# Last attention's scores in three fp32r passes instead of one fp32 product, with query and key split

## The reference, cut to what matters

```python
Q = query @ Wq + bq
K = key @ Wk + bk
V = value @ Wv + bv
Q = Q.reshape(B, S, NUM_KV, GROUPS, HEAD_DIM).transpose(0, 2, 3, 1, 4)
...
scale = 1.0 / jnp.sqrt(jnp.asarray(HEAD_DIM, query.dtype))
scores = jnp.einsum('bhgqd,bhkd->bhgqk', Q, K) * scale
w = jax.nn.softmax(scores, axis=-1)
y = jnp.einsum('bhgqk,bhkd->bhgqd', w, V)
...
return y @ Wo + bo
```

## Time and profile before

| what | us |
|---|---|
| median of 3 runs | 1620.5 (1618.6 to 1621.03) |
| the profiled execution, its own time | 1619.05 |
| span of the profiled execution | 1617.3 |
| the last attention, from its first key product to the last product with the values | about 1398 to 1567 |

### The profile page before, as it was taken

One profiled execution on the slowest core, in us unless ns is written; L12 is line 12 of the kernel. 1 busy time (PEld: TensorE's weight loads), 2 busy tenths in 40 slices (PEclk: granted clock), 3 DMA queues, 4 the chain that ended last, 5 costly groups with the idle time before them and its releaser, 6 DMA issues.

```text
span 1617.3 us, 25912 instructions
## 1 busy us (share of the span) xinstructions
PE 1572.8 (97%) x8958; PEld 1264.1 (78%) x8958; DVE 981.2 (61%) x2633; ACT 742.1 (46%) x2151; POOL 399.3 (25%) x278
## 2 busy tenths in 40 slices
PE   8999999999999999999989999999999999899997
PEld 7888888888888888888875877868696788666556
DVE  6762663626636356363676774848576767756677
ACT  5442443424434244343433462735355332288873
POOL 3131320313203132032204300000001343376651
PEclk9999999999999999999999999999999999999999
DMA  5111111101111011110224000000001613000001
GB/s 179 54 43 34 59 45 41 42 29 55 42 52 42 29 55 42 52 43 30 79 79 195 14 1 14 0 13 0 0 1 41 223 52 107 14 14 14 1 1 53
DMA packets 34436, 76.22 MB, mean 47 GB/s; under 512 B 5569, under 2 KB 18497, under 8 KB 32193
## 3 DMA queue, kind: packets, MB, share of 16 engines
q1 hardware_dynamic: 34368, 75.36, 14.1%
HBM read 73.25 MB, written 2.10 MB: 47 GB/s over the span
## 4 chain that ended last, share of the span: by engine, by line
PE 78%; DVE 10%; ACT 5%; issue 3%; DVEq 2%; POOL 1%; DMA 1%; POOLq 0%; SPq 0%; ACTq 0%
PE banks L1183 11%; PE banks L1128 10%; PE banks L1101 9%; PE banks L1109 9%; PE banks L1333 9%; PE banks L1437 5%; PE banks L1239 4%; PE banks L1222 3%; PE banks L1409 3%; ACT p L978 2%; PE banks L1229 2%; PE banks L1540 2%; PE banks L1563 1%; PE banks L1357 1%; PE banks L1547 1%
## 5 line engine op out<-in xcount | busy, mean ns | idle before, releaser
L1183 PE MATMUL banks<-w_o,atT 128*128 128x512 f32 x720 | 180.2, 396 | 0.0
L527 POOL TENSOR_TENSOR w_q<-w_raw_q,w_q 128x1792 fp32r<-128x1792 f32 x15 | 61.1, 4070 | 479.6 <-ACT w_q L733 479.6
L1101 PE MATMUL banks<-cT,w_k 128*128 128x512 f32 x720 | 178.0, 396 | 0.0
L1128 PE MATMUL banks<-w_v,cT 128*128 128x512 f32 x768 | 176.6, 390 | 0.0
L1128 PEld LDWEIGHTS banks<-w_v,cT 128*128 128x128 f32 x768 | 143.9, 188 | 29.9
L1109 PE MATMUL banks<-xT,w_q 128*128 128x512 f32 x672 | 163.8, 394 | 0.7 <-ACT kT L723 0.7
L1874 DVE TENSOR_TENSOR sA<-banks,pbias 128x512 f32<-128x512 f32 x64 | 44.1, 690 | 186.5 <-PE banks L1222 185.8
L1183 PEld LDWEIGHTS banks<-w_o,atT 128*128 128x128 f32 x720 | 131.9, 188 | 25.7
L1101 PEld LDWEIGHTS banks<-cT,w_k 128*128 128x128 f32 x720 | 131.9, 188 | 25.6
L1109 PEld LDWEIGHTS banks<-xT,w_q 128*128 128x128 f32 x672 | 123.7, 188 | 26.1 <-ACT kT L723 1.1
L792 ACT ACTIVATE sA<-sA,nmA 128x128 f32<-128x128 f32 x256 | 99.5, 393 | 56.9 <-DVE nmA L1879 56.6
(11 more groups left out here) (280 smaller groups left out, 3273.7 us busy)
## 6 DMA issues: line engine op xcount, KB each, us to landing
w_raw_v<-in_w0v SPq DMA_DIRECT2D x8, 1024.0 KB, 4.8
w_raw_q<-in_w0q SPq DMA_DIRECT2D x16, 512.0 KB, 3.3
w_raw_k<-in_w0k SPq DMA_DIRECT2D x15, 512.0 KB, 3.5
w_raw_o<-in_w0o SPq DMA_DIRECT2D x15, 512.0 KB, 3.3
cTp<-in_ctxT SPq DMA_DIRECT2D x12, 512.0 KB, 4.0
wq_raw<-in_wq SPq DMA_DIRECT2D x1, 3072.0 KB, 10.4
wo<-in_wo SPq DMA_DIRECT2D x1, 3072.0 KB, 20.1
x_res<-in_x SPq DMA_DIRECT2D x4, 512.0 KB, 11.3
```

The lines of the kernel that those rows point to most:

```text
L527: pool.tensor_tensor(w_part[slot][1][:], w_raw[slot][:], w_part[slot][0][:].bitcast(F32), ALU.subtract).then_inc(S(f"w{slot}_lo"), 1)
L1101: mm = pe.matmul(dst, wk_[l][:, c, h * P:(h + 1) * P], cT[r][:, c, half * HT:(half + 1) * HT], start=c == 0 and n == 0, stop=c == DC - 1 a ...
L1128: mm = pe.matmul(dst, cT[l][:, c, b * P:(b + 1) * P], wv_[r][:, c, :], start=n == 0, stop=n == 3 * DC - 1)
L1183: mm = pe.matmul(dst, atT[l][:, h, t], w[r][:, h, :], start=n == 0, stop=n == 5)
```

## The change

The scores are formed in three passes of fp32r (`PASSES`): high query by high key, high query by low key, low query by high key, each pass for the upper and then for the lower rows, all six into the two banks of the unit. For this, the queries and the block-diagonal keys exist twice, as a part rounded to fp32r and as the rest (`q3_lo`, `kbd_lo`). The new tiles lie on memory that is free in this stage.

- PE: six fp32r matmuls of 64x512 instead of two of fp32. They wait once for both halves' exponentials of unit U-2, where before each half waited for its own. Where PE waited for `q3_ready` it waits for `q_lo`, which DVE signals.
- ACT: line 969 drops the scale and writes fp32r. The number of its instructions stays.
- DVE: a new `queries_lo`, two instructions of 128x256 for each two query groups, that is twice for each pair. `keys` is now a rounded copy of 128x256, its rest of 128x256, and four products with the mask of 128x512 instead of two instructions of 128x512. The scale 1/4 is in the mask, and the small instruction that scaled the bias is gone.

```diff
-            pool.memset(kmask[:], 1.0)
+            pool.memset(kmask[:], float(HD3) ** -0.5)
...
-                                           bias=bq3[:, g:g + 1], scale=float(HD3) ** -0.5)
+                                           bias=bq3[:, g:g + 1])
...
-                        pe.wait_ge(S("q3_ready"), 2 * i + g // 2 + 1)
-                    for half in range(2):
-                        rows = slice(half * HALF3, (half + 1) * HALF3)
-                        if U > 1:
-                            pe.wait_ge(S("x3_e"), 2 * (U - 2) + half + 1)
-                        pe.matmul(banks2[2 - U % 2][:, half, :], q3[rows, i % 2, g, j * P:(j + 1) * P], kbd[rows, i % 2, j],
-                                  start=True, stop=True).then_inc(S("x3_s"), 1)
+                        pe.wait_ge(S("q_lo"), Q_LO_1 + 2 * i + g // 2 + 1)
+                    if U > 1:
+                        pe.wait_ge(S("x3_e"), 2 * (U - 2) + 2)
+
+                    for n, (l, r) in enumerate(PASSES):
+                        for half in range(2):
+                            rows = slice(half * HALF3, (half + 1) * HALF3)
+                            mm = pe.matmul(banks2[2 - U % 2][:, half, :], (q3, q3_lo)[l][rows, i % 2, g, j * P:(j + 1) * P],
+                                           (kbd, kbd_lo)[r][rows, i % 2, j], start=n == 0, stop=n == len(PASSES) - 1)
+                            if n == len(PASSES) - 1:
+                                mm.then_inc(S("x3_s"), 1)
...
-                        pe.wait_ge(S("kv3_ready"), 4 * i + 6)
+                        pe.wait_ge(S("kv3_ready"), 4 * i + 5)
...
-                    for j in range(2):
-                        dve.scalar_tensor_tensor(out=kbd[:, i % 2, j], in0=bank(6)[:, j * P:(j + 1) * P].unsqueeze(1)
-                                                 .to_broadcast([P, KV3 // 2, P]),
-                                                 scalar=bk3[:, 0:1], in1=kmask2[:].unsqueeze(2).to_broadcast([P, KV3 // 2, P]),
-                                                 op0=ALU.add, op1=ALU.mult).then_inc(S("kv3_ready"), 1)
+                    src = bank(6)[:, 0:PT2]
+                    dve.tensor_scalar(k3[0][:].bitcast(F32R), src, bk3[:, 0:1], None, ALU.add)
+                    dve.drain()
+                    dve.scalar_tensor_tensor(out=k3[1][:], in0=src, scalar=bk3[:, 0:1], in1=k3[0][:], op0=ALU.add,
+                                             op1=ALU.subtract).then_inc(S("kv3_ready"), 1)
+                    dve.drain()
+                    for l, dst in enumerate((kbd, kbd_lo)):
+                        for j in range(2):
+                            e = dve.tensor_tensor(dst[:, i % 2, j],
+                                                  k3[l][:, j * P:(j + 1) * P].unsqueeze(1).to_broadcast([P, KV3 // 2, P]),
+                                                  kmask2[:].unsqueeze(2).to_broadcast([P, KV3 // 2, P]), ALU.mult)
+                    e.then_inc(S("kv3_ready"), 1)
+
+                def queries_lo(i, g0, b):
+                    dve.wait_ge(S("q3_ready"), 2 * i + g0 // 2 + 1)
+                    for g in (g0, g0 + 1):
+                        e = dve.scalar_tensor_tensor(out=q3_lo[:, i % 2, g, :], in0=bank(b)[:, (g % 2) * PT2:(g % 2 + 1) * PT2],
+                                                     scalar=bq3[:, g:g + 1], in1=q3[:, i % 2, g, :].bitcast(F32), op0=ALU.add,
+                                                     op1=ALU.subtract)
+                    e.then_inc(S("q_lo"), 1)
...
                 keys(0)
                 values(0)
+                queries_lo(0, 0, 7)
                 ln_stats(2)
...
                 row_max(1, 1)
+                queries_lo(0, 2, 6)
                 sums(0, 1)
...
+                    if i + 1 < NPAIR and u == (2 if i == 0 else 1):
+                        queries_lo(i + 1, 0, 7)
+                    if i + 1 < NPAIR and u == 3:
+                        queries_lo(i + 1, 2, 7)
                     if i == 0:
                         first_pair(u)
```

More of the change, by code:

```diff
@@ L61 @@
 PARTS = {L1X: 0, L1F: 1, L2X: 2, L2F: 3}
+Q_LO_1 = 2 * KV1 * NPAIR
 BUSY = 13
@@ L221, in build @@
         xs = sb(ctx_b, "xs", [P, 2, 2, D])
+        ctx_g = ExitStack()
+        q3_lo = sb(ctx_g, "q3_part1", [P, 2, G3, PT2], F32R)
+        ctx_g.close()
         qTs = sb(ctx_b, "qTs", [P, 2, DC, PT2], F32R)
         wd3_hi = sb(ctx_b, "wd3_0", [P, IC3, D], F32R)
+        ctx_g = ExitStack()
+        k3 = [sb(ctx_g, f"k3_{l}", [P, PT2]) for l in range(2)]
+        ctx_g.close()
         eg = sb(ctx_b, "eg", [P, 2, I3])
@@ L327, in build @@
         kmask2 = sb(ctx_p, "kmask2", [P, KV3 // 2])
-        kbd = sb(ctx_p, "kbd", [P, 2, 2, KV3 // 2, P])
-        q3 = sb(ctx_p, "q3", [P, 2, G3, PT2])
+        kbd = sb(ctx_p, "kbd", [P, 2, 2, KV3 // 2, P], F32R)
+        q3 = sb(ctx_p, "q3", [P, 2, G3, PT2], F32R)
         p3 = sb(ctx_p, "p3", [P, 3, KV3, P])
@@ L336, in build @@
         rsc = sb(ctx_p, "rsc", [P, 2, 2])
+        ctx_g = ExitStack()
+        kbd_lo = sb(ctx_g, "kbd_part1", [P, 2, 2, KV3 // 2, P], F32R)
+        ctx_g.close()
         sg = sb(ctx_p, "sg", [P, 2, I3])
@@ L340, in build @@
         iq = sb(ctx_p, "iq", [P, 2, I3])
+        iT = sb(ctx_p, "iT", [P, 2, IC3, P], F32R)
         ami = sb(ctx_p, "ami", [P, 2])
@@ L1064, in _ @@
             pairs_ahead(act, lambda i, last: store_next(L2F, i, last))
-            act.wait_ge(S("scaled"), 3)
+            act.wait_ge(S("x3_ld"), 7 * 16)
             x3_act()
             def round_inner(i):
-                act.wait_ge(S("scaled"), (4, 6, 7)[i])
+                act.wait_ge(S("scaled"), (3, 5, 6)[i])
                 for j in range(2):
@@ L1073, in round_rows @@
             def round_rows():
-                act.wait_ge(S("scaled"), 5)
+                act.wait_ge(S("scaled"), 4)
                 for j in range(2):
@@ L1406, in scores @@
                         if h % 2 == 0 and b == 0:
[L1407 removed]
+                            pe.wait_ge(S("q_lo"), 8 * i + 2 * kv + h // 2 + 1)
                         for n, (l, r) in enumerate(PASSES):
@@ L1577, in attend @@
                     if U % U3 == G3 and i + 1 < NPAIR:
-                        pe.wait_ge(S("q3_ready"), 2 * i + 4)
+                        pe.wait_ge(S("q_lo"), Q_LO_1 + 2 * i + 4)
                     elif U % U3 == G3:
@@ L1595, in fill_first @@
                         if u == 3:
-                            pe.wait_ge(S("q3_ready"), 3)
+                            pe.wait_ge(S("q_lo"), Q_LO_1 + 3)
                         x3_queries(1, 2 * u - 4, 2 * u - 2, 7)
@@ L1606, in fill_early @@
                     if u == 2:
-                        pe.wait_ge(S("q3_ready"), 2 * i + 3)
+                        pe.wait_ge(S("q_lo"), Q_LO_1 + 2 * i + 3)
                         x3_queries(i + 1, 2, 3, 7)
```

5 lines of the change are left out of this document (1 added, 4 removed).

## The result

| | before | changed |
|---|---|---|
| median, us | 1620.23 | 1630.99 |
| lowest to highest, us | 1618.6 to 1621.03 | 1627.03 to 1631.32 (4 runs) |
| profiled execution (its span), us | 1619.05 (1617.3) | 1627.03 (1625.3) |

The ratio is 1.0066, with a 95% interval of 1.0053 to 1.0079: the change costs 9 to 13 us. The forecast was 1625.0 us in a range of 1617 to 1630. The direction was right, and the time lies just above the range.

What follows compares the result with a forecast made beforehand. The prediction took PE as the bound, with DVE and ACT holding the chain in two stretches. Its terms, -4.9 + 1.4 + 1.2 + 3.9 + 2.8 = +4.4 us, gave about 1625 us against the median, range 1617 to 1630.

Steps and rivals of the forecast that it cites:

- The scores: PE's scores in the last attention: 0.79 us a unit instead of 1.06, 18 x 0.27 = -4.9 us.
- rival 4: Row halves do not overlap in fp32r: 1.48 us for a unit's scores, +7.6 instead of -4.9, near 1637; chance 0.05.
- The start: Stage's start: DVE's longer keys and wait for ACT's queries delay statistics and row maxima, +1.4 us (0 to 2).
- evidence against a fall: Stage's start, against rival 1: PE idle for 3.3 of 13.5 us there, yet a granted clock of 1.00.
- Pair 0: Longer keys at u = 4 delay unit 7's row maximum by 2.3 us and more; +1.2 us (0 to 2).
- Pair 1: From 1464, queries_lo waits for ACT ahead of statistics; y and PE's key product come later, +3.9 us (2 to 4.5).
- The step that failed: Behind pair 1's key product, longer keys shift row maxima by 5, but PE catches up: nothing more than the 3.9.
- Pair 2: From 1504.7, the same chain without the weight split delays y: +2.8 us (1.5 to 3.5).
- rival 1: New waits for y in pairs 1 and 2 both drop PE's clock: +3.6 us, some 1628.6; chance 0.12.
- The end: Behind unit 23: five pieces of shorter scores, 5 x -0.27 = -1.4 us; no new DVE work in the last pair.
- Rival 2: Half of DVE's 9.3 us is absorbed: -4.9 + 4.7 = -0.2, 1620.3, no change; chance 0.24.
- Rival 3: Faster: only the start's loss is real, -4.9 + 1.4 = -3.5, about 1617.0; chance 0.13.

Runs made afterwards that it cites:

- PE's part alone: Changed kernel with keys as before, no rests of queries, high parts in all three fp32r passes; 0.9980 of the kernel before, 3.2 us faster.
- DVE's part alone: Changed kernel with all new DVE work and waits, but scores in fp32 as before; 1.0055 of the kernel before, 8.9 us over it.

## Why the prediction was right in its sign and short in its size

**The scores: right mechanism, size off.** Forecast 0.79 us a unit, measured 0.89. The records of one unit of the changed kernel:

```profile
1476.91 0.50 PE L1576 MATMUL banks<-kbd,q 64*128 64x512 f32 x2
1477.24 0.39 PE L1576 MATMUL banks<-kbd_part,q 64*128 64x512 f32 x2
1477.47 0.40 PE L1576 MATMUL banks<-kbd,q_part 64*128 64x512 f32 x2
1477.80 1.09 PE L1585 MATMUL banks<-ident,p 128*128 128x128 f32 x8
```

The pairs start 0.33 and 0.23 us apart, and the transposes follow 0.33 after the last. So a pass is 0.23 as taken, but the extra of about 0.1 is there twice, ahead of the second pair and behind the last. The prediction had found 0.20 of extra in the old 1.06 and carried only half of it over. The term is 18 x 0.17 = 3.1 us instead of 4.9, and PE's part alone gave 3.2. That the row halves overlap held, so rival 4 fell. The rule of strict program order (the Trainium skill, "TensorE: Matmul & The Clock Gate", "Part 3: Packing small matmuls") does not describe these records: with the halves issued one after the other they run side by side all the same.

**The start: the number is in part luck.** +1.4 forecast, +1.5 measured at unit 4. The reason held: with the statistics first, the loss was gone in the trace. But its size was about 0.7 us, as in the repeated run. The rest is the clock, at the very place that the prediction had named as evidence against a fall. PE idled for 3.35 us ahead of unit 2, and the transposes behind it took 1.97 us instead of 1.09:

```profile
1415.12 1.97 PE L1585 MATMUL banks<-ident,p 128*128 128x128 f32 x8
```

and the window shows the clock at 0.50:

```profile
1415.00:1418.00 3.00, 3.00 (x18) 2.55 (x20) 2.12 (x5) 2.45 (x11) 2.55 (x4) 0.50 0.01 3
```

**Pair 0: short.** Forecast +1.2, measured 0.8 + 6 x 0.17 = 1.8. In the chain shown above, `kbd` and `kbd_part` hold DVE from 1439.66 to 1442.54, the row maximum and ACT's exponentials follow, and `xn` begins at 1445.15. PE's timeline:

```profile
1450.88 1.09 PE L1585 MATMUL banks<-ident,p 128*128 128x128 f32 x8 [1.09 <-ACT xnT L864]
```

The late row maximum does not only use up the work in hand. It pushes `xn` and ACT's copy `xnT`, and PE waits 1.09 us for that. The kernel with the keys' split and no rests waits 1.10 us at the same place.

**Pair 1: the big term somewhat too large, the step behind it wrong.** `y` began at 1479.83 against 1475.09 in the earlier trace rows, 4.7 later, of which 1.66 had come in with ACT's copy (1466.04 against 1464.38 in the earlier trace rows). So the new order lost 3.1 of its own; 3.9 was forecast, in bounds of 2 to 4.5. DVE's timeline shows it as it was drawn:

```profile
1466.91 0.88 DVE L2241 SCALAR_TENSOR_TENSOR q_part<-banks,bq,q 128x256 fp32r<-128x256 f32 x2 [1.86 <-ACT q L980]
1467.88 1.29 DVE L1865 BATCH_NORM_STATS2 stat<-x_res 128x6 f32<-128x512 f32 x2
...
1478.12 0.88 DVE L2241 SCALAR_TENSOR_TENSOR q_part<-banks,bq,q 128x256 fp32r<-128x256 f32 x2 [0.55 <-ACT q L980]
1478.91 0.99 DVE L2200 TENSOR_SCALAR xh<-x_res,mv,rstd 128x512 bf16<-128x512 f32 x2
1479.83 0.68 DVE L2265 COPY y<-banks 128x512 f32<-128x512 f32 x1
```

and PE's key product had idled for it:

```profile
1480.56 2.00 PE L1536 MATMUL banks<-cTp,wk 128*128 128x256 f32 x8 [1.67 <-DVE y L2265]
```

**The step that failed** is the sentence behind this term: that PE "then catches up with work in hand of 2 to 3 us: nothing more". From unit 15 to unit 20 PE should have won 1.4 us; it lost 0.8, 2.2 on the wrong side. It is the mechanism of pair 0 again, and the prediction had put it at nothing for the keys of pairs 2 and 3. The keys ran from 1482.78 to 1487.17, 4.4 us where 3.7 were forecast; behind them came the row maximum, ACT's exponentials, `xn` (2.12 us) and `xnT`, and PE waited 0.65 us at 1494.81 and 0.20 at 1500.56. I had counted on PE's work in hand there, because the kernel before was bound by PE. The delay of `y` ahead of it is not needed for the loss. In the kernel with the keys' split and no rests, PE waited only 0.47 us for `y` ahead of the key product, and behind the keys it still has

```profile
1491.06 1.09 PE L1585 MATMUL banks<-ident,p 128*128 128x128 f32 x8 [0.66 <-ACT xnT L864]
1496.81 3.70 PE L1551 MATMUL banks<-wo,y 128*128 128x512 f32 x8 [0.20 <-DVE y L2265]
```

The traces give the change by stretch, each from the first key product of the stage and against the kernel before ("again" is the repeated run of the changed kernel):

| stretch | changed | again | scores alone | with the keys' split | DVE's part alone |
|---|---|---|---|---|---|
| up to unit 4 | +1.5 | +0.7 | -0.2 | -0.2 | +1.6 |
| to unit 10 | +0.8 | +0.8 | -1.0 | +0.5 | +1.2 |
| to unit 15 | +2.9 | +3.6 | -1.2 | -0.2 | +3.0 |
| to unit 20 | +0.8 | +0.8 | -0.5 | +1.0 | +1.0 |
| to unit 23 | +3.8 | +3.7 | -0.1 | -0.1 | +2.3 |
| to the end | -1.3 | -0.6 | -1.2 | -0.1 | -0.3 |

The columns "scores alone" and "with the keys' split" differ by 1.5 us up to unit 10, by 1.5 up to unit 20 and by 1.1 behind unit 23. These are the stretches behind the key splits of pairs 1, 2 and 3, so each of the three puts its row maxima on the path. Another 0.9 lies in the stretch up to unit 15. By the medians the split costs 4.2 us, where the prediction had only the 1.2 of pair 0. The same step is also seen from the other side: DVE's terms (9.3 forecast, 8.9 measured with the old scores) were about right in sum, and the -4.9 beside them was not there, because behind the keys as well as ahead of the key products PE waits for what it wins.

**Pair 2: the delay right, and the clock on top.** +2.8 was forecast, and the stretch lost 3.8. PE's timeline:

```profile
1524.54 3.45 PE L1536 MATMUL banks<-cTp,wk 128*128 128x256 f32 x8 [2.83 <-DVE y L2265]
```

and the window of this product (busy time of each engine, granted clock, DMA):

```profile
1524.50:1528.00 3.50, 3.46 (x12) 2.58 (x16) 1.42 (x4) 2.88 (x16) 3.50 (x5) 0.57 0.00 0
```

PE idled for 2.83 us, and the granted clock was 0.57 in this window, so mostly at 1.2 GHz. The eight products took 3.45 us instead of 2.00 in pair 1: 1.5 us. Without them the stretch lost 2.3, as it did in the kernel with DVE's part alone, where the clock did not fall. This is rival 1 in one of its two places. In the other run of this kernel the clock fell in both pairs, in pair 1 ahead of the wait for `y` and not behind it.

**The end: the number is luck.** 1.3 us came back behind unit 23, and the sum has 1.4 there. But five units of scores give only 0.8, and the keys of pair 3 cost about 1.1 there. What made up for it is that the kernel before had a low clock at 1555, which cost 1.8 us by the prediction's own reckoning, and this execution had none there.

**The sum.** In the trace: +1.5 + 0.8 + 2.9 + 0.8 + 3.8 - 1.3 = +8.5, less 0.5 from ahead of the stage = +8.0. The stage by itself cost 8.5, which is 4.1 more than the +4.4 forecast. By terms, with 0.17 for each of the 18 pieces: PE's gain 3.1 instead of 4.9 (+1.8), the start +0.1, pair 0 (0.8 + 6 x 0.17) +0.6, pair 1 (2.9 + 2 x 0.17) -0.6, behind it (0.8 + 5 x 0.17) +1.7, pair 2 and its clock +1.0, the end (-1.3 + 5 x 0.17) -0.5; that is 4.1. By the medians the cost is 10.7 and 9.1 us; the range ended at 1630 because it let the clock cost 3.6 us only on top of a sum that was too small.

**The rivals.** Rival 2 (half of the delays are absorbed) was wrong: DVE's part alone cost 8.9 of the 9.3 us of its terms. Rival 3 (faster) would have needed under 1.7 us of DVE's work on the path; the keys alone put over 4 us there. What stays open is how much of the median is the clock, since a trace shows one execution. The runs give an estimate: the mean granted clock was 0.991 to 0.996 in the eight executions of the changed kernel, 0.994 in the mean, and 0.998 in those of the kernel before. Among the eight, 0.001 less goes with some 0.9 us more, so the 0.004 between the kernels would go with 3 to 4 of the 9 to 11 us. No experiment holds the clock fixed, and with DVE's part alone 8.9 us were lost at mean clocks of 0.995 to 0.999.

## What to carry to other kernels

A wait written into an in-order engine costs not the work behind its semaphore but all that is queued behind it: here about half of the cost of a new 0.9 us step was standing still for an operand, in front of statistics that did not need it. Put such a step where its operand is long there, and follow the delay on both sides of the engine, to the buffer that it frees and to the next reduction that feeds another engine. A gain on the engine that binds is worth its trace value only while that engine stays the one that binds: 3.2 us by itself, nothing beside 9 us of new work elsewhere.

## What the runs showed of the hardware

**Products out of SBUF stretch beside POOL.** The four `kbd` and `kbd_part` products of a pair have one shape, yet took from 677 to 1523 ns. The records of the changed kernel behind the key products at 1438, 1482 and 1528 (least, median, most ns; first and last start):

```profile
L2233 DVE TENSOR_TENSOR kbd<-k,kmask x2: 677/881/1085, 1439.7 to 1440.7; 128x512 fp32r<-128x512 f32 x2
...
L2233 DVE TENSOR_TENSOR kbd<-k,kmask x2: 721/1122/1523, 1483.9 to 1484.5; 128x512 fp32r<-128x512 f32 x2
L2233 DVE TENSOR_TENSOR kbd_part<-k,kmask x2: 679/679/679, 1486.0 to 1486.6; 128x512 fp32r<-128x512 f32 x2
...
L2233 DVE TENSOR_TENSOR kbd<-k,kmask x2: 684/689/694, 1529.2 to 1529.8; 128x512 fp32r<-128x512 f32 x2
```

and the timeline of POOL at those times:

```profile
1439.16 1.04 POOL L677 TENSOR_TENSOR p<-p,rs 128x512 f32<-128x512 f32 x1
...
1484.01 1.49 POOL L677 TENSOR_TENSOR p<-p,rs 128x512 f32<-128x512 f32 x1
...
1527.98 1.04 POOL L677 TENSOR_TENSOR p<-p,rs 128x512 f32<-128x512 f32 x1
```

The long ones are those that meet a multiplication of POOL's: at 1439.66 one that runs until 1440.2, and 1085 ns; at 1484.5 one that runs until 1485.5, and 1523 ns, with POOL's own taking 1.49 instead of 1.04. Where POOL is idle, 677 to 694 ns. The old `keys` read one operand from PSUM and took 720 to 751 ns every time, with a multiplication of POOL's beside them too (from 1438.18, the keys from 1438.04). The Trainium skill, page "SBUF — State Buffer", section "SBUF: two separate sides", says that a DVE operation with two SBUF inputs and a POOL operation that reads SBUF exclude each other for a whole instruction; these records agree, with 0.4 us added in pair 0's keys and 0.85 in pair 1's. No experiment was made for this, but the others move the two engines against each other, and the long products go with the overlap. Without the rests of the queries the multiplication starts 0.95 us ahead of the `kbd` products of pair 0 (1438.35 and 1439.30), and the two take 1.29 us instead of 1.69. With DVE's part alone, two operations of POOL's meet those at 1529.03, which take 2.16 us where the changed kernel has 1.29. It is a part of what made the keys longer than forecast.

**The same idle went with either level of the clock.** Four places, with PE's idle time ahead and the granted clock behind it:

| place | 0.50 to 0.57 | 1.00 |
|---|---|---|
| ahead of unit 2 | 3.35 us, changed | 3.34, the repeated run |
| ahead of the second query products of pair 1 | 1.34 and 0.34, the repeated run | 1.34 and 0.34, changed |
| ahead of the key product of pair 2 | 2.83, changed | 2.71, DVE's part alone |
| ahead of the projection in the last pair | 1.53, before | 1.53, changed |

So the idle time just ahead does not tell by itself whether the clock falls, not even for one and the same kernel, and a forecast has to carry both cases. What it costs is plain: eight products of 128x256 in 3.45 us against 2.00.
